# Layer-norm small operations for two slots at a time in a recurrent stage, and a new order of VectorE's work in an expert stage

## The reference

```python
x = x + _L0_gnn_ref(_layernorm(x), adj, W)           # relu of the normalised adjacency @ (x @ W.T)
x = x + _L0_ffn_ref(_layernorm(x)[None], ...)        # 8 experts, two per row
x = x + _L1_gnn_ref(_layernorm(x), adj, W, b)        # columns standardised, then adjacency
x = x + _L1_ffn_ref(_layernorm(x)[None], ...)        # 30 steps, below

# experts: for each e, weighted by the softmax of the two best gate scores
h = relu(x @ W1[e].T + b1[e])          # 256 -> 1024
y = h @ W2[e].T + b2[e]                # 1024 -> 256

# 30 steps, each on all rows
h = h + 0.01 * tanh(h)
h = h * sigmoid(h)
h = layernorm(h, ln_w, ln_b)           # over the 256 features of a row
h = h @ W.T + b
```

## Time and profile before

| | us |
|---|---|
| median of 3 executions | 2172.43 (2172.1 to 2175.57) |
| the profiled execution | 2169.98 |
| its span | 2168.2 |
| experts, first to last layer-1 tile | 531 to 937 |
| steps stage | from about 1280 to the end |

### The profile page before, as it was taken

One profiled execution on the slowest core, in us unless ns is written; L12 is line 12 of the kernel. 1 busy time (PEld: TensorE's weight loads), 2 busy tenths in 40 slices (PEclk: granted clock), 3 DMA queues, 4 the chain that ended last, 5 costly groups with the idle time before them and its releaser, 6 DMA issues. The chain is left out here.

```text
span 2168.2 us, 46179 instructions
## 1 busy us (share of the span) xinstructions
PE 1847.8 (85%) x12658; PEld 1738.4 (80%) x12658; DVE 1655.9 (76%) x4066; ACT 1367.3 (63%) x2758; POOL 1125.8 (52%) x2479
## 2 busy tenths in 40 slices
PE   3403999962999999957999979999999999999998
PEld 2303999962999999956999968888888888888887
DVE  7998666653888888845766648888888888888886
ACT  2302665542566566534655648888888888888885
POOL 1001021233555555533000019989898998989896
PEclk9855999985999999978999989999999999999999
DMA  7776567823777777731766500000000000000001
GB/s 270 268 269 217 180 170 178 208 83 121 224 219 219 223 221 218 223 92 36 242 185 185 161 16 2 2 2 0 2 2 2 1 2 2 1 3 1 3 2 64
DMA packets 108446, 245.12 MB, mean 113 GB/s; under 512 B 22113, under 2 KB 52579, under 8 KB 99820
## 3 DMA queue, kind: packets, MB, share of 16 engines
q1 hardware_dynamic: 93676, 225.21, 33.3%
q0 software_dynamic: 14592, 17.91, 4.4%
HBM read 223.30 MB, written 19.75 MB: 112 GB/s over the span
## 5 line engine op out<-in xcount | busy, mean ns | idle before, releaser
L575 ACT ACTIVATE g_hi<-g_raw 128x384 fp32r<-128x384 f32 (+1 forms) x468 | 236.4, 511 | 197.3 <-PE g_acc L938 192.8
L1743 DVE SCALAR_TENSOR_TENSOR ffn_u<-ffn_th,ffn_psH 128x512 f32<-128x512 f32 x390 | 266.0, 682 | 121.9 <-ACT ffn_th L1697 121.8
L791 DVE TENSOR_TENSOR g_lo<-g_raw,g_hi 128x384 fp32r<-128x384 f32 (+1 forms) x468 | 245.9, 542 | 142.5 <-ACT g_hi L575 140.1
L1670 PE MATMUL ffn_psH<-ffn_w2h,ffn_vTh 128*128 128x256 f32 x1080 | 327.9, 304 | 5.6 <-DVE ffn_vTl L1736 5.6
L938 PE MATMUL g_acc<-g_hi,g_sh 128*128 128x384 f32 (+1 forms) x936 | 313.6, 335 | 16.5 <-DVE g_lo L791 16.4
L938 PE MATMUL g_acc<-g_lo,g_sh 128*128 128x384 f32 (+1 forms) x936 | 309.5, 331 | 0.0
L938 PE MATMUL g_acc<-g_hi,g_sl 128*128 128x384 f32 (+1 forms) x936 | 309.3, 330 | 0.0
L1670 PE MATMUL ffn_psH<-ffn_w2l,ffn_vTh 128*128 128x256 f32 x1080 | 305.0, 282 | 0.0
L1670 PE MATMUL ffn_psH<-ffn_w2h,ffn_vTl 128*128 128x256 f32 x1080 | 304.7, 282 | 0.0
L1775 POOL TENSOR_SCALAR ffn_vn<-ffn_vn,ffn_rstd,ffn_shift 128x256 f32<-128x256 f32 x540 | 297.8, 555 | 0.0
L1731 DVE BATCH_NORM_STATS2 ffn_stats<-ffn_vn 128x6 f32<-128x256 f32 x780 | 281.6, 404 | 14.6 <-issue 14.6
(11 more groups left out here) (214 smaller groups left out, 4820.8 us busy)
## 6 DMA issues: line engine op xcount, KB each, us to landing
g_raw<-in_adjt SPq DMA_DIRECT2D x208, 384.0 KB, 4.7
deg_ring<-in_adjt SPq DMA_DIRECT2D x104, 384.0 KB, 5.2
moe_w1raw<-in_wall SPq DMA_DIRECT2D x33, 1024.0 KB
moe_w2raw<-in_wall SPq DMA_DIRECT2D x33, 1024.0 KB, 5.6
g_raw<-in_adjl SPq DMA_DIRECT2D x26, 256.0 KB, 4.2
moe_b<-in_eb SPq DMA_DIRECT2D x33, 128.0 KB
x<-in_x SPq DMA_DIRECT2D x1, 3328.0 KB, 11.8
deg_ring<-in_adjl SPq DMA_DIRECT2D x13, 256.0 KB, 3.7
```

The lines of the kernel that those rows point to most:

```text
L575: act.activation(hi[:, split_slot(m, j), 0:w], raw[:, c, q * w:(q + 1) * w], ACT.Copy).then_inc(hi_done, 1)
L791: dve.tensor_tensor(lo[:, b, 0:w], raw[:, c, q * w:(q + 1) * w], hi[:, b, 0:w].bitcast(F32), ALU.subtract).then_inc(lo_done, 1)
L1670: last = pe.matmul(psH[w % R][:, q * D:(q + 1) * D], a[:, w % R, q * KD + k, :], b[:, k, :], start=(k == 0 and j == 0), stop=(k == KD - 1 ...
L1743: dve.scalar_tensor_tensor(out=u[:, a], in0=th[:, a], scalar=0.01, in1=psH[a][:], op0=ALU.mult, op1=ALU.add).then_inc(u_done, 1)
```

## The change

In the expert stage a list `ORDER = (0, 2, 1, 3)` gives the order in which the chunks of the first matrix are split, on ScalarE and on VectorE. VectorE makes `xl` of the next tile before the four chunks of `wl` instead of behind them (the very first tile keeps its order). TensorE waits for two chunks before block 0 and for all four before block 4, instead of for all four at the start.

In the steps stage the smalls `veps`, `mr`, `rstd` and `shift` are made for two slots by one instruction of four columns, when the second slot of a pair (an odd one) has its statistics. Their buffers hold two steps (`2 * NT` columns), since 13 slots are an odd number. The normalisation of both slots of a pair waits for the pair's `shift`. `FOUR_PASS` shrinks from four groups of a step to two.

```diff
+        ORDER = (0, 2, 1, 3)
...
-            for c in range(NCH):
+            for c in ORDER:
                 split_high(act, c, 0)
...
-                        split_high(act, hb // 2, o)
+                        split_high(act, ORDER[hb // 2], o)
...
                 if ahead:
-                    for k in range(NCH):
-                        dve.wait_ge(wh_done, t * NCH + NCH + k + 1)
-                        split_low(k, o)
                     dve.wait_ge(xh_done, t + 2)
                     dve.tensor_tensor(xl[:], psX[:], xh[:].bitcast(F32), ALU.subtract).then_inc(xl_done, 1)
+                    for k, c in enumerate(ORDER):
+                        dve.wait_ge(wh_done, t * NCH + NCH + k + 1)
+                        split_low(c, o)
...
-                pe.wait_ge(wl_done, t * NCH + NCH)
                 for hb in range(HB):
+                    if hb % (HB // 2) == 0:
+                        pe.wait_ge(wl_done, t * NCH + (2 if hb == 0 else NCH))
...
-        FOUR_PASS = (1, 4, 7, 10)
+        FOUR_PASS = (3, 9)
...
+        def column(m):
+            return m % (2 * G) * Q
+        def pair(m):
+            return slice(column(m - 1), column(m - 1) + 2 * Q)
+        def pairs(rounds, m):
+            return rounds * (BODY * G // 2) + m // 2 + 1
+        def closes(m, lag):
+            return chained(m, lag) and (m - lag) % 2 == 1
...
-                    act.wait_ge(shift_done, n - NORM + 1)
+                    act.wait_ge(shift_done, pairs(rounds, m - NORM))
...
-                if chained(m, STATS):
-                    q = tiles(m - STATS)
+                if closes(m, STATS):
+                    q = pair(m - STATS)
                     wait_apart(pool, aggr_done, n - STATS + 1, passed)
                     pool.tensor_scalar(veps[:, q], mv[:, q, 1], 1.0, LN_EPS, ALU.mult, ALU.add).then_inc(eps_done, 1)
-                if chained(m, SHIFT):
-                    q = tiles(m - SHIFT)
-                    pool.wait_ge(rstd_done, n - SHIFT + 1)
+                if closes(m, SHIFT):
+                    q = pair(m - SHIFT)
+                    pool.wait_ge(rstd_done, pairs(rounds, m - SHIFT))
                     pool.tensor_tensor(mr[:, q], mv[:, q, 0], rstd[:, q], ALU.mult).then_inc(mr_done, 1)
                 if chained(m, NORM):
-                    wait_apart(pool, shift_done, n - NORM + 1, passed)
+                    wait_apart(pool, shift_done, pairs(rounds, m - NORM), passed)
...
-                if chained(m, STATS):
+                if closes(m, STATS):
...
-                    pool.tensor_tensor(rstd[:, q], veps[:, q], g.mhalf[:, 0:Q], ALU.pow).then_inc(rstd_done, 1)
+                    pool.tensor_tensor(rstd[:, q], veps[:, q], g.mhalf[:, 0:2 * Q], ALU.pow).then_inc(rstd_done, 1)
-                if chained(m, SHIFT):
+                if closes(m, SHIFT):
```

More of the change, by code:

```diff
@@ L1193, in split_low @@
                                   ALU.subtract).then_inc(wl_done, 1)
-            for c in range(NCH):
-                dve.wait_ge(wh_done, c + 1)
+            for k, c in enumerate(ORDER):
+                dve.wait_ge(wh_done, k + 1)
                 split_low(c, 0)
@@ L1539, in steps_block @@
         stats = sb("ffn_stats", [P, NT, 6])
[L1540 to L1544, removed]
+        mv = sb("ffn_mv", [P, 2 * NT, 2])
+        veps = sb("ffn_veps", [P, 2 * NT])
+        rstd = sb("ffn_rstd", [P, 2 * NT])
+        mr = sb("ffn_mr", [P, 2 * NT])
+        shift = sb("ffn_shift", [P, 2 * NT])
         vn = sb("ffn_vn", [P, NT, D])
@@ L1703, in slot @@
                     t = (m - NORM) % G * Q + 1
-                    act.wait_ge(shift_done, n - NORM + 1)
-                    act.activation(vn[:, t, :], vn[:, t, :], ACT.Identity, scale=rstd[:, t:t + 1],
-                                   bias=shift[:, t:t + 1]).then_inc(vn2_done, 1)
+                    s = column(m - NORM) + 1
+                    act.wait_ge(shift_done, pairs(rounds, m - NORM))
+                    act.activation(vn[:, t, :], vn[:, t, :], ACT.Identity, scale=rstd[:, s:s + 1],
+                                   bias=shift[:, s:s + 1]).then_inc(vn2_done, 1)
             run(act, slot)
@@ L1748, in slot @@
                         t = (m - STATS) % G * Q + q
-                        last = dve.bn_aggr(mv[:, t, :], stats[:, t, :])
+                        last = dve.bn_aggr(mv[:, column(m - STATS) + q, :], stats[:, t, :])
                     last.then_inc(aggr_done, 1)
@@ L1770, in slot @@
                     pool.tensor_tensor(mr[:, q], mv[:, q, 0], rstd[:, q], ALU.mult).then_inc(mr_done, 1)
                 if chained(m, NORM):
-                    wait_apart(pool, shift_done, n - NORM + 1, passed)
+                    wait_apart(pool, shift_done, pairs(rounds, m - NORM), passed)
                     for q in range(1 if (m - NORM) % G in BY_ACT else Q):
                         t = (m - NORM) % G * Q + q
-                        last = pool.tensor_scalar(vn[:, t, :], vn[:, t, :], rstd[:, t:t + 1], shift[:, t:t + 1],
+                        s = column(m - NORM) + q
+                        last = pool.tensor_scalar(vn[:, t, :], vn[:, t, :], rstd[:, s:s + 1], shift[:, s:s + 1],
@@ L1776, in slot @@
                                                   ALU.mult, ALU.add)
                     last.then_inc(vn_done, 1)
-                if chained(m, STATS):
-                    q = tiles(m - STATS)
-                    pool.wait_ge(eps_done, n - STATS + 1)
-                    pool.tensor_tensor(rstd[:, q], veps[:, q], g.mhalf[:, 0:Q], ALU.pow).then_inc(rstd_done, 1)
-                if chained(m, SHIFT):
-                    q = tiles(m - SHIFT)
-                    wait_apart(pool, mr_done, n - SHIFT + 1, passed)
+                if closes(m, STATS):
+                    q = pair(m - STATS)
+                    pool.wait_ge(eps_done, pairs(rounds, m - STATS))
+                    pool.tensor_tensor(rstd[:, q], veps[:, q], g.mhalf[:, 0:2 * Q], ALU.pow).then_inc(rstd_done, 1)
@@ L1785, in slot @@
+                if closes(m, SHIFT):
+                    q = pair(m - SHIFT)
+                    wait_apart(pool, mr_done, pairs(rounds, m - SHIFT), passed)
                     pool.tensor_scalar(shift[:, q], mr[:, q], -1.0, 1.0, ALU.mult, ALU.add).then_inc(shift_done, 1)
```

## The result

| | median us | runs | ratio to the kernel before |
|---|---|---|---|
| before | 2172.26 | 4 | |
| changed | 2103.23 (2102.26 to 2103.84) | 4 | 0.9679 (0.9662 to 0.9696) |

The account below looks back on a forecast made before the run. GpSimd's own length was taken to bound the steps, a closed way to set the next slot; 55 us from steps plus 13 from experts made 68, so 2104 us. Its own range was 2090 to 2117, 8 in 10 2075 to 2132.

Parts of the forecast that it names:

- the four engine lengths: Steps slot if each engine waits for nobody: GpSimd 1.60, VectorE 1.89, TensorE 1.91, ScalarE 1.79 us; TensorE-bound rival 2072, chance 0.25.
- closed way: Steps: waits VectorE, GpSimd, ScalarE, back to VectorE's u three slots on, 5.85 us; new slot 1.99, 55 us saved.
- the hand-over from VectorE's aggregation to `veps`: Steps, part of the way: aggregation lasting 0.24 us plus 0.10 allowed to GpSimd's start.
- the allowance of no change: Steps loop turns: six, left at 3.3 us each; bounds 5 us saved or 14 lost.
- The other signs: Steps and experts: 195 of each small, GpSimd busy near 0.75, no xl wait; wrong if slot outside 1.91 to 2.06.
- release before the last matmul: Experts, tile change: xl and two chunks release TensorE at about 593.0, before its last matmul starts at 593.87.
- the second wait: Experts: TensorE's wait for four chunks before block 4, due 2.9 us after the start; VectorE there by 594.2.
- VectorE's slack: Experts: VectorE waits 1.65 us for a tile's first hr, so its length of some 10.8 us doesn't take over.
- The gap: Experts, TensorE at a tile change: 0.61 us between matmul starts against 0.12; removing it gives 15 us at most.
- the idle time: Experts: TensorE's 30 waits for xl, 12.1 us in all; the forecast took 13 us saved.
- The row's 0.12: TensorE's 256-column matmuls start 0.12 us apart, making its length 1.91 us a slot; by 109 ns, 1.79.
- the short slots: Steps: VectorE slots without a low part, 1.38 us against 1.98; each of four in 26 lies under a way.

Follow-up runs that it names:

- NORM 10: Changed kernel with NORM 10 instead of 9, so both engines normalise a group one slot later: 2055.71 us (0.9472 to the kernel before).
- NORM 10 on the old kernel: The kernel before the change with NORM 10 and nothing else: 2172.78 us (1.0016).
- The smalls first: Changed kernel with GpSimd's veps, power, mr and shift ahead of its normalisations: 2065.18 us (0.9499 to the kernel before).
- the extra small operation: Changed kernel with one more 128x4 GpSimd operation ahead of veps, into a buffer nobody reads: 2119.83 us (0.9773 to the kernel before).

## Why the prediction was right

**What bounds the kernel.** Right. The chain and the start-to-start distances on GpSimd gave 2.13 us a slot (26 slots of the kernel before take 55.46, which is 2.133), and NORM 10 on the old kernel changed nothing.

**The next pace.** The step that made the forecast was to look past the four engine lengths for a closed way. By the lengths the slot would have been 1.91 and the kernel 2072, 31 us too fast. The way was predicted at 5.85 us and 26 slots at 51.67; measured were 6.03 and 52.49. With 6.03 put in, the prediction's own sum is 52.39. The missing 0.18 are the hand-over from VectorE's aggregation to `veps`, 0.44 start to start instead of 0.34, 0.02 on `veps`, 0.03 on the power and `mr` (1.08 instead of 1.05), and 0.01 on each of three others. The smalls first and NORM 10 confirm it by making the way shorter or looser, the extra small operation by making it longer.

**The size of the steps' gain.** 55 forecast, 44.9 measured between the traces: the term mis-sized is the way's length, 0.03 us a slot or 12 us in 390. A turn costs 107.65 - 104.98 = 2.7 us instead of 3.2 (114.11 less twice the 55.46 of 26 slots before), so that the allowance of no change held to 3 us in six turns. 55 - 12 + 3 = 46 leaves 1 us.

**The power of four columns.** 1.02 forecast, 1.007 measured. The other signs came too: 195 of each small, GpSimd busy 0.73 of the stretch, no wait for `xl`, and a slot inside 1.91 to 2.06.

**The experts.** 13 forecast, 19.7 measured. The mechanism was right in each step: release before the last matmul, the second wait met, VectorE's slack enough. It still waits 0.6 us a tile for the first `hr`, of 1.65; of the difference 0.66 is the shorter tile, and 0.4 are its four copies `hh`, which take 0.60 us on the mean instead of 0.50. Two terms were too small. The gap was read at one tile as 0.61 and was 0.66 on the mean of 32, and 13 was set near the idle time, which doesn't hold the whole gap: (0.66 - 0.12) x 31 = 17 us. And after a wait the second matmul comes 0.21 behind the first instead of 0.12, 0.09 x 31 = 3 us, which the prediction didn't count.

**The sum.** The two misses, 10 too much and 7 too little, and 4 us of an early start that isn't the change's, cancel. That 2104 is so near to 2103.2 is luck.

**TensorE's pace.** The row's 0.12 held: three-pass slots take 1.875 us when TensorE is the bound. The prediction set the row against the 109 ns of the Trainium skill (TensorE: Matmul & The Clock Gate, Back-to-back issue gap) and said that the trace disagrees. That was misread. The section gives this formula for an isolated matmul; for a stream of weight loads and matmuls, as here, it has 81 ns at 128 columns and 131 ns at 512, and the 0.12 us at 256 lie between the two.

**FOUR_PASS.** The prediction counted the step from four plain groups to two as 0.05 us for TensorE and put its cost on VectorE into the short slots. In the changed kernel this step loses 6 us. It gains only once TensorE is the bound: 1.1 us in 26 slots with NORM 10.

## What to carry to other kernels

When engines run a pipeline written by hand, the slot is set by the longest engine or by the longest ring of waits, whichever is longer. For a ring, sum the start-to-start times once around and divide by the slots that it spans. Here the kernel before was held by an engine, and taking work off it gave 45 us where a looser ring gave nothing. The changed kernel was held by a ring, and there more lag for one stage (NORM 10: 45 us) or moving the ring's operations ahead of others on their engine (38 us) helped. Where a release waits for several operations together, reordering them does nothing unless the wait itself is split as well.

## What was not expected of the hardware

- TensorE after a wait: in the kernel before the second matmul of a tile starts 0.22 us behind the first on the mean of 32 tiles, and the later ones are 0.12 apart; without the wait, after the change, all are 0.12 apart.
- VectorE's copy of 128x512 from float32 to `fp32r` in the experts took 0.44 us at the median before and 0.61 after (109 and 114 of them between 560 and 900), with the same operands; the slowest were 0.70 and 0.71. No run separated the cause.
- GpSimd's power of 128 x n: 0.70 us for two columns, 0.96 for three, 1.01 for four, 1.34 for six, 1.64 for eight. Four cost hardly more than three.
